# Preln layer on eight cores: a new order for the last tile, the squares of q on ScalarE, the bias as a product of one row, and the norms fetched behind the second select

## The reference

```python
x = x + attn(layernorm(x))      # below
x = x + ffn(layernorm(x))       # out_real = xr @ Wr.T - xi @ Wi.T + bias_real, out_imag likewise

mixed = silu(causal_conv4(x @ W_qkv.T));  q, k, v = split(mixed, 3)
z = x @ W_z.T;  beta = sigmoid(x @ W_b.T)
g = -exp(A_log) * softplus(x @ W_a.T + dt_bias)
q = l2norm(q) * HD ** -0.5;  k = l2norm(k)
def step(S, (q_t, k_t, v_t, b_t, g_t)):
    S = S * exp(g_t) + outer(k_t, v_t * b_t)
    return S, q_t @ S
out = out * rsqrt(mean(out * out) + 1e-6) * silu(z)
return out @ W_out.T
```

## Time and profile before

| | us |
|---|---|
| runs | 872.6, 930.7, 861.51 |
| median | 872.6 |
| profiled execution | 864.25 |
| its span on the slowest core (0) | 862.7 |
| spans of cores 2, 4, 6 | 852.5, 860.0, 850.7 |
| spans of cores 1, 3, 5, 7 | 824.4, 828.1, 827.5, 829.3 |
| TensorE busy (share of the span) | 660.2 (77%) |
| VectorE, ScalarE, GpSimd busy | 474.1, 300.4, 277.8 |

### The profile page before, as it was taken

The page is one execution under the profiler, slowest core; times in us unless marked ns, Lnnn a source line. Parts: engine busy times, 40 slices in busy tenths (PEclk is TensorE's granted clock), DMA queues, the critical chain, the costliest instruction groups (busy, mean ns, idle before and its releaser), DMA issues.

```text
span 862.7 us, 13978 instructions; the slowest of 8 cores (824.4 to 862.7 us)
## 1 busy us (share of the span) xinstructions
PE 660.2 (77%) x4531; PEld 299.7 (35%) x4607; DVE 474.1 (55%) x655; ACT 300.4 (35%) x531; POOL 277.8 (32%) x317
## 2 busy tenths in 40 slices
PE   1868774699796989878798997789999994654552
PEld 1423321344343434433343443344444442221210
DVE  5349981356865466486546657744556543453431
ACT  3254331273541444344144443314544423221100
POOL 2111230222624225063332505424145334544210
PEclk9998987899997999999799999989999996776686
DMA  8997999867757677575666857566577676324221
GB/s 183 254 218 167 218 267 168 183 186 201 194 141 176 166 183 200 143 206 129 168 162 183 203 141 194 138 156 183 147 184 184 171 143 111 72 66 86 86 85 41
DMA packets 144543, 139.97 MB, mean 162 GB/s; under 512 B 90622, under 2 KB 107444, under 8 KB 144336
## 3 DMA queue, kind: packets, MB, share of 16 engines
q1 hardware_dynamic: 130512, 109.87, 49.5%
q0 software_dynamic: 13952, 29.12, 17.8%
HBM read 107.39 MB, written 23.25 MB: 151 GB/s over the span
## 4 chain that ended last, share of the span: by engine, by line
PE 47%; DMA 17%; DVE 15%; issue 9%; SPq 5%; ACT 5%; POOL 1%; DVEq 0%; ACTq 0%; POOLq 0%
PE pRG L506 16%; PE pRG L553 9%; PE pA L978 6%; PE pB L936 6%; DMA s_rb<-rscr 3%; PE pRG L936 3%; SPq L131 3%; DMA s_w<-wcat 2%; SPq L136 2%; DMA s_ktil<-s_post 2%; DMA s_w<-wscr 2%; ACT L410 1%; DVE s_dsb L797 1%; DMA dscr<-s_d 1%; DVE s_ktil L750 1%
## 5 line engine op out<-in xcount | busy, mean ns | idle before, releaser
L506 PE MATMUL pRG<-s_lnxT,s_w 128*128 128x512 bf16 x1241 | 304.6, 396 | 54.0 <-DMA s_w<-wcat 22.4
L506 PEld LDWEIGHTS pRG<-s_lnxT,s_w 128*128 128x128 bf16 x1280 | 125.7, 101 | 215.2 <-issue 82.0
L553 PE MATMUL pRG<-s_pre,s_d 128*128 128x512 bf16 x459 | 118.2, 390 | 15.9 <-DVE s_pre L533 13.1
L131 POOL DMA_DIRECT2D rscr<-s_ssb x40 | 22.8, 575 | 228.2 <-ACT s_pre L530 75.2
L558 ACT ACTIVATE s_post<-pRG 128x512 bf16<-128x512 f32 x120 | 69.0, 593 | 62.0 <-PE pRG L553 61.3
L533 DVE CAST s_pre<-pRG 128x512 bf16<-128x512 f32 x70 | 47.6, 685 | 49.6 <-PE pRG L506 49.2
L553 PEld LDWEIGHTS pRG<-s_pre,s_d 128*128 128x128 bf16 x480 | 42.2, 99 | 64.5 <-issue 20.2
L530 ACT CAST s_pre<-pRG 128x512 bf16<-128x512 f32 x50 | 29.2, 585 | 98.5 <-PE pRG L506 98.2
L978 PE MATMUL pA<-s_wbig,s_ln2T 128*128 128x512 bf16 x236 | 55.9, 388 | 9.1 <-DMA s_ln2T<-s_ln 8.8
L777 POOL TENSOR_SCALAR_AFFINE_SELECT s_dsb<-s_dsb 128x1024 bf16<-128x1024 bf16 x36 | 44.9, 1248 | 51.8 <-ACT s_dsb L773 51.3
L577 ACT ACTIVATE s_zT<-pRG 128x512 bf16<-128x512 f32 x40 | 23.9, 598 | 102.9 <-PE pRG L506 100.1
(11 more groups left out here) (151 smaller groups left out, 883.9 us busy)
## 6 DMA issues: line engine op xcount, KB each, us to landing
s_w<-wscr SPq DMA_DIRECT2D x128, 256.0 KB, 4.0
s_d<-dscr SPq DMA_DIRECT2D x96, 128.0 KB, 3.9
s_x<-x SPq DMA_DIRECT2D x22, 512.0 KB, 7.1
s_rb<-rscr POOLq DMA_DIRECT2D x40, 256.0 KB, 5.9
y<-s_x SPq DMA_DIRECT2D x20, 512.0 KB, 2.9
s_xa<-x SPq DMA_DIRECT2D x18, 512.0 KB, 5.8
s_w<-wcat POOLq DMA_DIRECT2D x32, 256.0 KB, 7.1
wscr<-s_w SPq DMA_DIRECT2D x32, 256.0 KB, 7.8
```

The lines of the kernel that those rows point to most:

```text
L131: lane.e.dma_start(out=out, in_=in_).then_inc(self.h, 16)
L506: ins = P.e.matmul(ps, w[:, dc * 128:(dc + 1) * 128], lnxT[u % 2][:, dc, :], start=(dc == 0), stop=(dc == 7))
L553: ins = P.e.matmul(ps, dr[i % ND][:, tap * 128:(tap + 1) * 128], pre[:, j, tap:tap + 512], start=(tap == 0), stop=(tap == 3))
```

## The change

Four edits.

1. `add_bias` goes, and with it the bias spread over 128 partitions. `s_brow` is one row: the bias (1,024 values) and 128 ones. `ffn` begins with two products of one row (L975 of the new kernel), ones by bias, and its sixteen others add to them.
2. The squares of q leave `qtil` (GpSimd) for `q_squares` (ScalarE), which stands right ahead of `oT`.
3. In the loop, `kscale` goes from behind `ln1_norm` to behind `qk(n, 1)`, and `r_load(n1)` from ahead of `decay(n, 1)` to behind it.
4. The last tile: the loop body is written in another order (below), the transposes of k and v are issued a chunk further ahead, `ln2_rstd` and `ln2_norm` of a chunk move into the next step, and the last chunk's `outproj`, norm, transpose and `ffn` are written in halves of 512 columns, with the transpose on TensorE (`out_last`, `ffn_last`).

```diff
+        def q_squares(n):
+            t, c = NPRE + n // 4, n % 4
+            S.need(silu_tok[(t, 7)], ss_tok.get(n - 1))
+            qsq_tok[n] = S.mark(S.e.activation(
+                out=qsq, in_=post[t % 2][:, c, 0:1024].rearrange("p (a b) -> p a b", a=8),
+                func=AF.Square))
...
-            P.need(l2_tok[n], ffnw[0])
+            P.need(late["bias"], late["ones"], l2_tok[n], ffnw[0])
+            for hf in range(2):
+                P.e.matmul(ps[:, hf * 512:(hf + 1) * 512], brow[:, 1024:1152],
+                           brow[:, hf * 512:(hf + 1) * 512], start=True, stop=False)
...
+        def out_last(n):
+            ps, fr = pair["C"]
+            P.need(*fr[0])
+            P.need(gat_tok[n])
+            bn = bnB[n % 2]
+            for hf in range(2):
+                hc = slice(hf * 512, hf * 512 + 512)
+                for cc in range(8):
+                    ins = P.e.matmul(ps[:, hc], buf("ga", n)[:, cc * 128:(cc + 1) * 128],
+                                     wout[:, cc, hc], start=(cc == 0), stop=(cc == 7))
+                V.need(P.mark(ins), x2ld_tok[n], norm2_tok.get(n - 2))
+                t = V.mark(V.e.tensor_tensor(out=x2[n % 3][:, hc], in0=ps[:, hc],
+                                             in1=x2[n % 3][:, hc], op=ALU.add))
+                V.need(t)
+                t = V.mark(V.e.bn_stats(out=bn[:, 6 * hf:6 * hf + 6], in_=x2[n % 3][:, hc]))
...
+            P.need(t, *psB_free[0])
+            pb = pB[:, 0:512].bitcast(BF16)
+            for dc in range(8):
+                ins = P.e.transpose(out=pb[:, dc * 128:(dc + 1) * 128],
+                                    in_=ln2[:, dc * 128:(dc + 1) * 128], identity=i128b)
+            V.need(P.mark(ins), ffn_tok.get(n - 2))
+            l2_tok[n] = V.mark(V.e.tensor_copy(
+                out=ln2T[n % 2], in_=pb.rearrange("p (a b) -> p a b", a=8)))
...
-                if att:
-                    kscale(g)
                 if on1:
                     r_load(n1)
-                if own:
-                    decay(n, 1)
-                if on2:
-                    add_bias(n2)
...
+        tvk(4 * NPRE + N0 + 1)
         for n in range(N0, N0 + 4):
...
             state_decay(g)
-            if more:
-                tvk(g + 1)
-            xr_load(n)
             oT(n, "C")
-            if more:
-                kscale(g + 1)
             state(g, "D")
             r_act(n)
+            if n > N0:
+                ln2_rstd(n - 2)
+                ln2_norm(n - 2)
+            gate_out(n - 1)
             if more:
                 decay(n + 1, 0)
-            gate_out(n - 1)
+                decay(n + 1, 1)
+                kscale(g + 1)
+                qtil(n + 1)
+                q_squares(n + 1)
+                if n < N0 + 2:
+                    i51_load(n + 2)
+                    tvk(g + 2)
+            xr_load(n)
             outproj(n - 1, "C")
             if more:
-                qtil(n + 1)
-                decay(n + 1, 1)
-                if n < N0 + 2:
-                    i51_load(n + 2)
+                qk(n + 1, 0)
+                qk(n + 1, 1)
             ln2_stats(n - 1)
...
```

91 lines of the change are left out of this document (50 added, 41 removed).

## The result

| | before | after |
|---|---|---|
| median of the runs, us | 876.1 | 836.9 |
| profiled execution | 864.25 | 837.8 |
| its span | 862.7 (core 0) | 836.2 (core 6) |
| streamed part: first product of attention to the last tile's first, cores 0, 2, 4, 6 | 549.0, 545.8, 546.4, 542.3 | 550.9, 548.6, 539.5, 552.6 |
| from there to the end, the same cores | 136.8, 134.2, 137.0, 133.9 | 104.5, 107.4, 108.2, 109.0 |

The ratio of the times is 0.965, with a 95% interval of 0.954 to 0.976: faster, by 3.5%. The forecast was 815 and the range reached to 838, so the time lies just inside its upper end, outside the 800 to 830 of the likeliest case, and 22 us above the forecast. The two lower rows of the table say where: the last tile is 28 us shorter, as forecast (30), and the streamed part is not shorter at all, where 19 us were forecast.

What follows compares the result with a forecast made beforehand. It took TensorE's waits to bound the streamed part and a chain of single steps through all engines the last tile. 862.7 - 19.3 (streamed part) - 30 (last tile) = 813.4, plus 1.55: 815 us; range 795 to 838.

Steps and rivals of the forecast that it cites:

- the likeliest case: Whole kernel: the forecast itself holds, 815 us, range 800 to 830; chance 0.58.
- the last tile: Last tile: shorter chunks through the new order and earlier transposes, and a shorter end: -2.5 -18 -9.5 = -30 us.
- (a): Streamed part, fourth chunks: without GpSimd's long operations and with k's scaling moved, attention waits less for L797: -18 us.
- (b): Streamed part: the convolution's waits (L553) for VectorE's copies, held by GpSimd, all go: -9.9 us.
- (c): Streamed part: with most waits gone, TensorE's slower clock after pauses is recovered: -6 us over three tiles.
- (d): Streamed part: squares of q on ScalarE, ahead of the squares of o, make TensorE wait: +8.6 us, between 0 and 17.
- (e): Streamed part: the bias as two one-row products per chunk, 0.22 us each at full price: +6 us.
- (f): Streamed part: norms are fetched 1 to 2 us later, behind the second select; their user also stands later: nothing.
- F: Norms arrive late, gate_out holds VectorE's queue and the output product waits for its bank: slower, about 880 us; chance 0.02.
- B: Streamed part: TensorE meets the next late thing, weights or squares of o; half to all of 19 lost: 825 to 836; chance 0.17.
- E: Edits cancel: the scaling of k is slow of itself and only changes place: about 855 us; chance 0.03.
- Rival C: Last tile keeps long chunks through late transposes and loads or a half clock: 823 to 832 us; chance 0.10.

Runs made afterwards that it cites:

- e9: Changed kernel with the squares of q in the loop back on GpSimd, right behind the first select: 826.8 us, ratio 0.949 to the kernel before.
- e11: Changed kernel without the one-row bias products, so the output lacks the bias: 827.5 us, ratio 0.952 to the kernel before.
- e2: Changed kernel without the fetches of the norms in the loop, except the first chunk's: 816.1 us, ratio 0.929 to the kernel before.
- e4: Changed kernel with norms of chunks 1 to 3 computed and stored half a step earlier, fetched at the next step's start: 806.6 us, ratio 0.913 to before.
- e7: Changed kernel with the last tile in the order of the kernel before: 855.9 us, ratio 0.987 to the kernel before.
- e12: Kernel before with norms of chunks 1 to 3 computed, stored and fetched half a step earlier: 840.8 us, ratio 0.968 to the kernel before.

## Why the prediction was right and where it failed

**(a), (b): the waits named went, the time did not.** L829's wait for L797 fell from 25.7 to 2.4, L750 to 1.21, L553's wait for the copies from 9.9 to 0.3 (core 0). That GpSimd holds these operations was read rightly from the earlier trace rows; that a held one stays held until GpSimd pauses is not so in every row (below). But on core 0 all of TensorE's waits in the stream sum to 69.4 before and 58.5 after, and its busy time rose by 10, from 477.6 to 487.4. The sum took a removed wait for removed time, with only the squares put against it. What would be late next was looked for in the tile that had run in 128.1 us; that tile has no long stall whose end could uncover a late fetch, and the next late things were a chunk's norms.

**(c) failed.** It took most pauses of TensorE to be gone; they moved. The granted clock of the tiles is 0.94, 0.98 and 0.97, and products behind the new waits run at 1.2 GHz (6.51 for 16): on core 0 the output products of the stream took 53.9 us before and take 61.0 now.

**(d) was right:** L888 waits 12.1 to 12.2 us where L883 waited 3.1, so 9 against 8.6; e9 shows 8 in the stream. One operation takes 1.057.

**(e) was too small:** about 10 us in e11 instead of 6. In the last tile's second chunk above, the sixteen products start 0.53 behind the first of the two, so a product of one row put the next off by 0.27, a little more than the 0.22 taken.

**(f) is the step that failed.** It put the later fetch at "Nothing". The fetch costs up to 14 us (e2) as the kernel stands, and the path of which it is the end, statistics, Ln and Exp, store, wait, fetch, gate_out, costs 39 (e4). The 14 of (f), the 6 of (c) that did not come and the 4 by which (e) was too small make about the 22 us that are missing; they overlap, so this is a rough account. What had kept the fetch from being late are these two rows of the kernel before, core 0, in the second fourth chunk of the earlier trace rows:

```profile
555.46 1.44 POOL L131 DMA_DIRECT2D s_rb<-rscr  x2
...
564.37 1.21 DVE L920 TENSOR_TENSOR s_gated<-s_og,s_rb 128x1024 bf16<-128x1024 bf16 x1
```

The fetch had 8.9 us to land before gate_out came up, 5.99 of them L750. In the changed kernel it leaves at 263.15 and VectorE is ready for gate_out at 263.29, when L750 ends. The forecast counted the 6 us a chunk as gained in (a), and in (f) it still took the user of the fetch to stand 1.2 later than before. Three more readings were missing. The landing time was taken over all chunks (5.9 in the median), but a fourth chunk's fetch is used 5 to 11 us after it leaves, with VectorE waiting for it, and there the slack is least. The start of the fetch was taken as "1 to 2 us later"; in three of core 0's four fourth chunks it waits 2.0 to 3.0 for its own store on top. And the slack of 1.5 was read in a second chunk and taken for all sixteen.

**The rivals.** F named the mechanism exactly (gate_out holds VectorE's queue, L853 stands behind it, the output product waits for its bank), and had 2 chances in 100. It was held to be all or nothing, in each of 16 chunks; it works in the five waits where the fetch is late and costs up to 14 us there. B all but gave the size (825 to 836 against 836.9), by the right rule that TensorE meets the next late thing, but named weights and the squares of o; the weights' wait rose by no more than 1 us. Against B stood the 128.1 us tile, which was no evidence. E's first part, that L750 only changes its place, is wrong.

**The last tile was right:** 28 against 30 us, of which the new order is 22 and the other edits 6 (e7). On the pages' cores, the first chunk gained 0.4 (forecast 2.5), the second 6.7 and the third 9.8 (9 each), the end 10.9 (9.5); from the last chunk's first product (783.94) to the end of the last add (828.91) 45.0 us passed (45 to 46). The second chunk's missing 2.3 is one row: gate_out takes 3.43 instead of 1.2, since in the new order it starts just as GpSimd begins its two selects. Rival C (long chunks) did not come; the output products take 4.8 to 5.2, as counted.

**One operation held over several, but not always.** L925 starts at 752.96, 0.2 ahead of the first select, and ends at 756.39, 1.1 behind the end of the second: its own work comes after both. It is the forecast's reading of the 5.99 in the earlier trace rows, where L750 starts 0.7 ahead of GpSimd's three operations and ends 1.1 behind the last. The Trainium skill (SBUF — State Buffer, Who interferes with whom) has the shared pair of ports held for one whole instruction; by that, L925 would have come in between the selects, at about 2.4 (an estimate). The rows of e12 agree with the page: there L750 came in behind one select and ahead of the bias add. Even in the kernel before, the L750 ahead of the wait at 265 took 4.20 (from 259.48) and came in ahead of the decay of the state, which took 2.01 instead of 1.03. So both happen in this case, what decides between them was not found, and "held until GpSimd pauses" is no rule.

## To carry to other kernels

A removed wait is only removed time if what is next in line is early enough in that same chunk; read the slack in the chunk that had the stall, not in a neighbour or in a mean over all. Before a long operation is taken from a queue, see what it was covering there: if the instruction behind it waits for a store to land, that wait comes to light when the long operation goes. In both kernels here a chain of small steps that ends in a round trip through memory was better off at the end of the step in which its input is ready, with the table load that comes with it, than at the head of the next one, where everything waits for the engine that does it.

## What the runs showed of the hardware that was not expected

A round trip through memory took, in a fourth chunk, 17 us from the store's issue to the use of what was fetched (256.76 to 273.98); the shortest fetch landed in 3.5. A small VectorE operation that meets GpSimd's can be held as long as a large one: e12 shows the copy of 128x9 elements at 0.17, at 3.18, by nothing but when it comes. The same scaling of k was held over three GpSimd operations (5.99) and, in e12, over one (2.10), where GpSimd's add behind it took 1.0 longer. And a table load of 1.28 us with two activations of 0.7 and their store, none of which stands in TensorE's list of waits under its own name, was worth about 15 us in one kernel and 17 in the other by being moved.
